# Attention and FFN layer on 8 cores: the loads and stores of the xt buffers move from SyncE's queue to GpSimd's

## The reference

```python
xn = _layernorm(x, axis=-1)
x = x + _L0_attn_ref(xn, wq, wk, wv, wo, pope_bias) + _L0_ffn_ref(xn, ...)
# attention: 16 heads of 64; q_mag, k_mag = softplus(xn wq^T), softplus(xn wk^T)
# q_embed, k_embed = (mag * cos, mag * sin) of the position, 2*64 wide
out = softmax(q_embed k_embed^T / 8) v ;  out @ wo^T
# ffn: global gate gf from the mean over tokens, then three cycles of
tf = sigmoid(gelu(gelu(gelu(o @ w1) @ w2) @ w3) @ w4)
o = o + (0.1 + 0.2 * 2 * (0.7 * gf + 0.3 * tf - 0.5)) * twist(o)
```

## Time and profile before

| | us |
|---|---|
| median of 2 runs | 4079.49 (4078.71 to 4080.27) |
| the profiled execution | 4074.24 |
| its span on core 7, first to last instruction | 4072.7 |
| spans of the 8 cores | 4054.2 to 4072.7 |
| busy in the span: PE, ACT, DVE, POOL | 2660.8, 1643.9, 1403.6, 40.5 |
| mean granted TensorE clock | 0.80 |

### The profile page before, as it was taken

One profiled execution on the slowest core, in us unless ns is written; L12 is line 12 of the kernel. 1 busy time (PEld: TensorE's weight loads), 2 busy tenths in 40 slices (PEclk: granted clock), 3 DMA queues, 4 the chain that ended last, 5 costly groups with the idle time before them and its releaser, 6 DMA issues.

```text
span 4072.7 us, 35741 instructions; the slowest of 8 cores (4054.2 to 4072.7 us)
## 1 busy us (share of the span) xinstructions
PE 2660.8 (65%) x10486; PEld 1086.2 (27%) x10486; DVE 1403.6 (34%) x2359; ACT 1643.9 (40%) x2082; POOL 40.5 (1%) x80
## 2 busy tenths in 40 slices
PE   0437776677767967567523576777767787766664
PEld 0213222232222223223212222232223222323322
DVE  5353233313332323333346333323332242233333
ACT  2205665566656022122123465666556701222221
POOL 0000000000000000000000000000000000000000
PEclk9958988899888578678766788998889856777777
DMA  6540011000100031120233011001110003022121
GB/s 152 130 86 23 13 27 26 16 13 24 27 17 5 22 98 67 48 91 34 82 104 116 24 26 26 16 11 26 26 25 15 7 10 81 32 93 73 42 83 57
DMA packets 84371, 193.23 MB, mean 47 GB/s; under 512 B 25559, under 2 KB 28632, under 8 KB 84184
## 3 DMA queue, kind: packets, MB, share of 16 engines
q1 hardware_dynamic: 73240, 175.74, 14.1%
q0 software_dynamic: 10944, 15.21, 2.7%
HBM read 134.27 MB, written 41.94 MB: 43 GB/s over the span
## 4 chain that ended last, share of the span: by engine, by line
PE 47%; DVE 22%; DMA 12%; issue 11%; ACT 5%; SPq 1%; DVEq 1%; POOL 0%; ACTq 0%; POOLq 0%
PE ps_w L170 24%; PE ps_s L170 15%; PE ps_pv L170 8%; DVE stream L170 6%; DMA xt<-x 4%; ACT pt L170 3%; DMA tmp<-qmag 3%; DMA xt<-ffn_s 2%; DVE vp L170 2%; DVE qh L170 2%; DVE ke L170 1%; SPq L170 1%; DMA ke<-kmag 1%; DMA w1t<-cnw 1%; DVE tmp L170 1%
## 5 line engine op out<-in xcount | busy, mean ns | idle before, releaser
L170 ACT ACTIVATE pt<-ps_s,cpool 128x1024 bf16<-128x1024 f32 x1024 | 1085.5, 1113 | 816.0 <-PE ps_s L170 812.3
L170 PE MATMUL ps_pv<-pt,vp 128*65 128x512 bf16 x2048 | 663.4, 408 | 289.9 <-DVE tmpB L170 228.4
L170 PE MATMUL ps_s<-qh,ke 128*128 128x512 bf16 x2048 | 663.7, 408 | 102.7 <-ACT pt L170 79.6
L170 PEld LDWEIGHTS ps_pv<-pt,vp 128*65 128x65 bf16 x2048 | 236.2, 118 | 572.0 <-issue 382.1
L170 PEld LDWEIGHTS ps_s<-qh,ke 128*128 128x128 bf16 x2048 | 174.3, 103 | 472.7 <-issue 395.1
L170 ACT ACTIVATE h<-ps_w,b1f 128x512 bf16<-128x512 f32 x192 | 131.9, 687 | 351.7 <-PE ps_w L170 351.7
L170 PE MATMUL ps_w<-ofm,w1t 128*128 128x512 bf16 x1024 | 255.3, 413 | 10.7 <-ACT ofm L170 10.7
L170 ACT CAST ofm<-ps_w 128x128 bf16<-128x128 f32 x256 | 49.6, 279 | 454.3 <-PE ps_w L170 454.2
L170 PE MATMUL ps_w<-ident,sbf 128*128 128x128 bf16 x512 | 64.7, 306 | 241.8 <-DVE sbf L170 241.8
L170 DVE COPY rowstg<-ps_pv 1x1024 f32<-1x1024 f32 x32 | 39.1, 1222 | 451.7 <-PE ps_pv L170 451.5
L170 DVE CAST vp<-ps_w 128x64 bf16<-128x64 f32 x512 | 115.8, 226 | 181.6 <-PE ps_w L170 153.8
(11 more groups left out here) (116 smaller groups left out, 2699.4 us busy)
## 6 DMA issues: line engine op xcount, KB each, us to landing
xt<-x SPq DMA_DIRECT2D x128, 512.0 KB, 4.0
ffn_s<-xt SPq DMA_DIRECT2D x32, 512.0 KB, 2.6
xt<-ffn_s SPq DMA_DIRECT2D x32, 512.0 KB, 4.0
out<-stream SPq DMA_DIRECT2D x32, 512.0 KB, 2.9
ke<-kmag SPq DMA_DIRECT2D x32, 256.0 KB, 4.0
qh<-qmag SPq DMA_DIRECT2D x32, 256.0 KB, 4.1
tmp<-qmag SPq DMA_DIRECT2D x32, 256.0 KB, 3.7
wqt<-wqT_s SPq DMA_DIRECT2D x16, 256.0 KB, 2.8
```

The lines of the kernel that those rows point to most:

```text
L170: inst = getattr(engine, op.method)(*op.args, **op.kwargs)
```

## The change

At six places the queue of a DMA becomes "gpsimd": the x loads of both loops of `gen_ln`, of `gen_wo` and of `gen_ffn`, and the ffn_s load and the out store of `gen_final`. Each load gets a new first key, so that its semaphore is one per place and buffer (`lnl`, `wol`, `ffl`, `fnl`), with the buffer's key kept for the dependences. The stores to `ffn_s` in `gen_wo` and the gcw1 loads into xt in `gen_gc` stay on SP's queue. The core of the diff (the first hunk stands twice, once for each loop of `gen_ln`):

```diff
@@ gen_ln, both loops @@
-                dma("sync", xb_t[:], x_d[s, tb * 128:(tb + 1) * 128, :], reads=["dx"], writes=[xb])
+                dma("gpsimd", xb_t[:], x_d[s, tb * 128:(tb + 1) * 128, :], reads=["dx"],
+                    writes=[f"lnl{tb % 2}", xb])
@@ gen_wo @@
-                dma("sync", xb_t[:], x_d[s, tb * 128:(tb + 1) * 128, :], reads=["dx"], writes=[xb])
+                dma("gpsimd", xb_t[:], x_d[s, tb * 128:(tb + 1) * 128, :], reads=["dx"],
+                    writes=[f"wol{tb % 2}", xb])
@@ gen_ffn @@
-                dma("sync", xb_t[:], x_d[s, tb * 128:(tb + 1) * 128, :], reads=["dx"], writes=[xb])
+                dma("gpsimd", xb_t[:], x_d[s, tb * 128:(tb + 1) * 128, :], reads=["dx"],
+                    writes=[f"ffl{tq % 2}", xb])
@@ gen_final @@
-                dma("sync", xb_t[:], ffn_s[s, tb * 128:(tb + 1) * 128, :],
-                    reads=["partD0", "partD1"], writes=[xb])
+                dma("gpsimd", xb_t[:], ffn_s[s, tb * 128:(tb + 1) * 128, :],
+                    reads=["partD0", "partD1"], writes=[f"fnl{tq % 2}", xb])
...
-                dma("sync", out_d[s, tb * 128:(tb + 1) * 128, :],
+                dma("gpsimd", out_d[s, tb * 128:(tb + 1) * 128, :],
```

## The result

| | before | after |
|---|---|---|
| median of the runs, us | 4080.63 (4077.91 to 4207.93, 10 runs) | 4144.17 (4121.97 to 4256.32, 11 runs) |
| ratio | | 1.0113 (95%: 1.0081 to 1.0145) |
| the profiled execution, us | 4074.24 | 4128.44 |

The changed kernel is 1.1% slower, 33 to 59 us, about 46. The forecast was 4112 us in a range of 4070 to 4160. The sign is right, and the size is some 15 us short.

The account below looks back on a forecast made before the run. PE held 47% of the chain, DVE 22%, transfers 12%, with loads in series at quarter ends. Terms 53.7 + 0.9 - 10.1 - 6.9 - 8 + 3 = +32.6 us gave a median of 4112 us, range 4070 to 4160.

Parts of the forecast that it names:

- Price of a POOL load: Loads on the chain, quarter ends and norms: 1.05 us more each in gen_final, 0.95 elsewhere; +53.7 us (35 to 68).
- landing part: From DMA start to landing, a POOL load takes 0.5 us longer than one from SP, the cast's 0.33 set apart.
- First x loads early: Start of item 0's norm: x loads on POOL no longer stand behind constants and the last sbdup transfer; -10.1 us.
- No queueing behind the stores of wT: Item 0's norm: x loads no longer wait behind SP's wT stores, which wait for DVE's cast; -6.9 us.
- Weights first: Start of the FFN: POOL issues 16 weight loads before x loads, so weights have the DMA engines; -8 us (0 to -10).
- Rival C: FFN start: x loads come so late that wo matmuls' PSUM buffers wait for DVE; -8 turns +4, 4124 us; chance 0.15.
- DVE beside descriptor writing: Quarter ends: DVE's stream operation holds up POOL's descriptor writing, twice per end at 6 ends; +3 us (0 to 10).
- rival A: POOL loads land after 6.3 us under load, set by descriptor writing; about 4207 us, slower by over 2%; chance 0.10.
- The last store: End of the program: the last out store, moved to POOL's queue, adds +0.9 us.
- Item 1's norm: First pass: 7 x loads on the chain at 0.95 us more each; second pass stays covered at 3.04 us a tile.
- B: A POOL load costs only its release, 0.43 us; 4075 us or a little less, 4065 at the lowest; chance 0.15.
- The chain doesn't get longer at all: Loads prefetched further ahead on POOL would leave the chain no longer; excluded for gen_final, since the stores moved too.

Follow-up runs that it names:

- e9: Kernel before with out stores, gen_ln's x loads and the x loads of gen_ffn's first quarter of each item on POOL's queue; 4000.0 us, ratio 0.9758.
- e5: Kernel before with only the out stores on POOL's queue, every load on SP's; 4010.2 us, ratio 0.9845.
- e11: Kernel before with out stores on POOL, loads on SP with the changed kernel's semaphores, series of load and add kept by waits; 4076.3 us, ratio 0.9966.
- e12: Kernel before, all on SP's queue, each next ffn_s load issued ahead of the out store, still waiting for the add; 4074.5 us, ratio 0.9982.
- e2: Changed kernel with gen_final's loads and stores back on SP's queue, all x loads on POOL's; 4064.0 us, ratio 0.9944 to the kernel before.
- e3: Changed kernel with out stores back on SP's queue, series of load and add kept by a wait; 4093.8 us, ratio 1.003 to the kernel before.
- e4: Changed kernel with out stores back on SP's queue and no added wait; 4010.9 us, ratio 0.982 to the kernel before.
- e10: Changed kernel with each next ffn_s load issued ahead of the out store, series kept, both on POOL; 4103.9 us, ratio 1.0025 to the kernel before.
- e1: Kernel before with only gen_final's loads and stores on POOL's queue, all x loads on SP's; 4115.5 us, a single run.
- e6: Kernel before with the out stores and the x loads of gen_ln on POOL's queue, the rest on SP's; 4007.1 us, ratio 0.9838.
- e7: Kernel before with out stores on POOL, series kept by waits, xt loads sharing a semaphore with the places ahead; 4130.1 us, ratio 1.0116.

## Why the prediction was right in sign, and short in size

**1. Price of a POOL load** (forecast 1.05 in `gen_final`, 0.95 elsewhere; bounds 0.65 and 1.25): the mechanism was right, the size low. The release part, 0.43, holds: 0.49 to 0.54 of issue where SP has 0.04. The landing part, 0.5, was one number for two cases. It is 0.1 to 0.2 for a load with no store near it (e9, item 1's norm), and 0.67 for ffn_s (4.28 to 4.95) and 1.26 for the first x load (4.42 to 5.68), both behind a store. The step grew by 1.29 us for 1.05, close to the upper bound (1.25, and 0.1 for the store), and the first x load by more than it. I took it from POOL's weight loads against SP's x loads, which differed in the cast; the right row to ask was one of a load behind a store on the same queue, and the trace had none. "Below zero excluded" stands. Over the 6 ends this is 45.1 for 39.

**2. First x loads early** (-10.1): right, and read too large from one core. On the 8 cores the first sum starts 8.7 us sooner on average; core 7, from which I had 35.25, was among the latest. 1.4 us are missing.

**3. No queueing behind the stores of wT** (-6.9): mis-sized. From the first sum to the last `xnb` the stretch is 1.1 us longer, and five loads at 0.95 would make 4.75, so by the forecast's own price 3.6 is what came of it; by the 0.6 that a lone POOL load costs here (0.45 of release, 0.1 to 0.2 of landing), only 2. No run separates the two. Another 1.2 was lost until the end of the attention (7.6 to 6.4). The stretch as a whole gave 6.4 for 12.2.

**4. Weights first** (-8): right in kind, 5.8. Rival C, that the weight burst gives nothing, falls: the last w1t to the first end is unchanged (+0.1).

**5. DVE beside descriptor writing** (+3): 0.25 us where it meets, so 3 us for the 12 places, as taken. No row stood behind the 3, so that it was hit is luck. The upper end of 10 us, which rival A leaned on, did not come, since POOL waits only for what is left of DVE's 0.81 us.

**The last store** (+0.9): wrong, see below. It costs 5.0 us.

**Item 1's norm**: its first pass cost about what was said (+8.8 for 9.8 with the end ahead of it), but by two misses that cancel. The end ahead of it and the load behind its last store cost more than forecast; from the first to the last sum the pass is 4.4 us longer (41.8 to 46.2), where six loads at 0.95 would make 5.7, and its pieces are no longer than before (4.14 and 4.21). The second pass stayed covered. Timeline of DVE, changed kernel:

```profile
2189.19 0.80 DVE L170 TENSOR_SCALAR xnb<-xt,mstat,rstat 128x1024 bf16<-128x1024 f32 x1
...
2195.28 0.80 DVE L170 TENSOR_SCALAR xnb<-xt,mstat,rstat 128x1024 bf16<-128x1024 f32 x1
```

Two tiles take 6.09 us, as the 6.08 of the earlier trace rows.

**The rivals.** A (6.3 us of landing for every load) falls: the median is 4.8 at worst. Its place was right, though: a piece behind a store reaches 7.14. B (release part only) is true of the x loads that run alone and false of the 31 behind a store, which decide. The 0.4 us of first byte that I cited from the Trainium skill, DMA: Bandwidth & Descriptors, shows in no landing of a lone load here (4.2 and 4.1 in e9, 4.1 and 3.9 in item 1's norm); what the trace has is the 0.5 us ahead of the DMA.

So the terms that failed are the landing part of term 1 (6 us at the ends), term 3 with 2 (6 us), the last store (4 us) and the weights (2 us), all in one direction, with 1 us back at item 1.

**Of the excluded case.** "The chain doesn't get longer at all" was rightly excluded because the stores moved with the loads. e5 and e11 show the other side of that sentence. Putting loads and stores on different queues is worth 1.5%, and this comes from the series alone: with the series kept (e11) the time is that of before.

## What to carry to other kernels

When a transfer is moved to another queue, look first at what stands ahead of it there. A store that waits for compute holds every load behind it, and taking just the store to a second queue gave 1.5% here, while taking both along cost 1.1%. Price a move by the pair (this kind of load behind that kind of neighbour), not by the median landing of the queue: here the same load cost 0.1 to 0.2 us of landing alone and 0.67 behind a store. And when an experiment adds a wait to keep an order, look in its timeline whether the wait brought others with it, before its time is believed.

## What was unexpected

**The end of the program.** From the end of the last DVE add to the end of the span it is 3.0 to 3.6 us with the last out store on SP (before, e12, e2, e3, e4), and 8.0 to 10.2 with it on POOL: 8.0 in after and e10, where POOL's queue has all x and ffn_s loads, 9.3 in e1 and e6, 10.0 in e9, and 10.2 in e5, e7 and e11, where of these transfers it has only the stores. Within a kernel with the store on POOL the cores agree to 0.01 us. The changed kernel, its last add and last store, and the DMA engines from 4117.5 to 4126.7 in 40 slices of 0.23 us:

```profile
4117.50 1.23 DVE L170 TENSOR_TENSOR stream<-stream,xt 128x1024 f32<-128x1024 f32 x1 [5.84 <-DMA xt<-ffn_s]
4119.30 0.54 POOL L170 DMA_DIRECT2D out<-stream  x1 [6.01 <-DVE stream L170]
...
DMA  0000000000004999991000000000000000000000
```

The data are through by about 4122, and the span goes on for 4.7 us. In the kernel before, whose last 4.3 us have this row, it is 0.7 us:

```profile
DMA  0000000000000000000389699889799310000000
```

What runs in that time no row shows. e9 with its last store on SP might be some 5 to 7 us faster; that was not tried.

**A POOL load behind a POOL store** lands 0.45 us later than one issued ahead of it, with an idle gap of 0.8 to 1 us in the DMA engines between the two; on SP's queue the order is worth 0.03 us. Part of it, some 0.20 us, is there with the store on SP's queue too (e3).
